# A factorization network for 2048 rows: layer 0's last tile halved and stacked, tile kinds and side work at other steps

## The chip, the cores and the metric

One core of a Trainium2 chip. The time is the device time of one execution in microseconds; the number compared is the median over several executions. Engines: TensorE (PE; PEld are its weight loads), VectorE (DVE), ScalarE (ACT), GpSimd (POOL), and SyncE (SP), which here only issues DMAs.

## The reference, cut to what matters

39 embedding tables are looked up for 2048 batch rows, 16 numbers each. Three layers (L0 to L2) then multiply every field of x0 with every field of xk and contract the pairs with a weight matrix; an MLP ends it.

```python
e = stack([tbl_f[ids[:, f]] for f in range(39)], axis=1)        # 2048 x 39 x 16
x0 = xk = e
for idx, (W, b) in enumerate([(w0, b0), (w1, b1), (w2, b2)]):   # W: 39 x fk x 128
    z = relu(einsum('bhd,bkd,hks->bsd', x0, xk, W) + b[None, :, None])
    if idx != 2:
        xk = z[:, :64, :]; direct.append(z[:, 64:, :])
    else:
        direct.append(z)
h = concatenate([sum(concatenate(direct, axis=1), axis=-1), dense_ctx], axis=1)
h = relu(h @ W_top1 + b_top1); h = relu(h @ W_top2 + b_top2); y = h @ W_top3
```

## The kernel before

**Turns and tiles.** A turn works on 128 batch rows and 8 of the 16 channels, so on 1024 columns; there are 32 turns (CHUNKS), two to a group of 128 rows. A tile is a block of up to 128 pair products (partitions) by 1024 columns; TensorE contracts it with a 128 x 128 block of weights into PSUM, in two halves of 512 columns. A turn has 47 steps, one tile each: steps 0 to 19 (PAIRED) are layer 1, steps 20 to 26 (SQUARED) are layer 0 of the turn that follows, steps 27 to 46 (LAST) are layer 2. All engines walk through the same list of steps (`turns`, L195), each emitting what it has to do at each step; the semaphores alone decide when it happens.

**Kinds.** The string PLAN (L58) gives each tile a letter. F: the fp32 product goes to TensorE as it is (L1014). V, D and P tiles are split: ScalarE rounds the product into `high` (L801), the rest `low = product - high` is subtracted by VectorE (V, D; L869) or by POOL (P; L638), and TensorE does three contractions, low weights by high, high weights by high (`contract`, L1014) and, LATE = 2 steps later, high weights by low (`contract_low`, L1049). The product of a D tile is made in PSUM, in the bank of the other accumulator; that of V and P tiles in SBUF. A V tile of 64 rows is stacked: its high part stands in partitions 0 to 63 and its low part in 64 to 127 of one buffer, its weights are there twice, and two contractions do for three, both two steps late (L1046, L1049). Before the change the stacked tiles are 19 and 46.

**Products (VectorE).** In layers 1 and 2 a product is a spread tile of x0 (SBUF) by the maps of the layer before (PSUM); two neighbours are made in one instruction where the plan allows (`pairs`; L914), else one (L918). Layer 0 is symmetric, so only shifts are needed: row s + 3 i of tile 20 + u is field i - s by field i + 3 u (L899), 117 rows a tile. Its 20 shifts fill 7 tiles, the last with two shifts. `prod` has 8 buffers and `high` has 4, so a product waits for TensorE's work on the tile 8 before.

**Side work at fixed steps.** The relus (`take`): layer 0 at RELU0_AT = 29, layer 1 at 21, each in three parts (L741 to L743), layer 2 at 3 (L725). The pair 27/28 needs relu 1, tile 0 of the next turn needs relu 0. The channel sums of `direct` (L925, L929, L936), three steps each: layers 0 and 1 from SUM01_AT = 27, layer 2 from SUM2_AT = 14. The low part of a V tile is emitted SUB = 3 steps after its product, that of a D tile SUB_D = 2. POOL also gathers table rows (L616), at steps that `gather_slots` spreads over those that are not P. In even turns TensorE transposes gathered rows at step 13 (L1056).

**Loads (SP).** `load_spread` (L540) fills the spread tiles in layer 2's steps; `load_first` at step 46 fills x_thrice (L530) and the first four `shifted` buffers (L518); tiles 24 to 26 of layer 0 are loaded into freed buffers (L518; L522 for the last one, two loads of 39 rows). In the start-up `load_thrice0` and `load_shifted0` do this in parts, as blocks of rows are written to DRAM.

Of the kernel before, what the change touches and what calls it, by code (L numbers as in the profile page):

```python
# [29 lines left out]
MAPS = 128  # L30
# [9 lines left out]
N0 = -(-SHIFTS // PER0)  # L40
N1 = -(-FIELDS // 2)
TILES = N1 + N0 + N1
TRIPLE = FIELDS * PER0
PERIODS = 2
# [13 lines left out]
PLAN = "FVFPPPFPFFDPFDVFFPFV" "FFFFFFF" "FPFFFVPFDPVFDPPDFPFV"  # L58
# [32 lines left out]
def shifts_of(u):  # L91

    return min(PER0, SHIFTS - PER0 * u)
# [115 lines left out]
def build(nc, a, out):  # L209
# [10 lines left out]
    with ctx:  # L220
# [27 lines left out]
        with nc.sbuf_tensor("shifted_r", [TRIPLE, RING0, COLS], f32r) as shifted_r, \  # L248
                nc.sbuf_tensor("x_thrice_r", [TRIPLE, COLS], f32r) as x_thrice_r:
            pass  # L250
        shifted = sb("shifted", [TRIPLE, RING0, COLS])
        x_thrice = sb("x_thrice", [TRIPLE, COLS])
# [33 lines left out]
        s_thrice = sem("s_thrice")  # L286
        s_shifted = [sem(f"s_shifted{u}") for u in range(N0)]
# [108 lines left out]
        w0_other = prod[0:TRIPLE, 4, 0:N0 * MAPS].rearrange("p (t s) -> p t s", s=MAPS)  # L396
# [85 lines left out]
        def _(sp):  # L482
# [5 lines left out]
            sp.dma_start(w_plain[0:TRIPLE, plan_f - PLAIN0:plan_f, :], a["w0_ab"][:, 0:PLAIN0, :]).then_inc(s_w0, 16)  # L488
            sp.dma_start(w0_other, a["w0_ba"]).then_inc(s_w0, 16)
            if PARTED0:  # L490
                sp.dma_start(parts_in[0:TRIPLE, plan_r - PARTED0:plan_r, :], a["w0_ab"][:, PLAIN0:N0, :]).then_inc(s_w0, 16)
# [23 lines left out]

            def load_shifted(n, u):
                if shifts_of(u) == PER0:
                    sp.dma_start(shifted[:, u % RING0, :], period(n, PER0 * u, FIELDS).unsqueeze(1).to_broadcast(  # L518
                        [FIELDS, PER0, COLS])).then_inc(s_shifted[u], 16)
                    return  # L520
                for s in range(shifts_of(u)):
                    sp.dma_start(shifted[s:TRIPLE - PER0 + s + 1:PER0, u % RING0, :], period(n, PER0 * u, FIELDS)  # L522
                                 ).then_inc(s_shifted[u], 16)
# [19 lines left out]
            for q in range(TURNED):  # L543
                sp.wait_ge(s_first_w[q], 16 * PERIODS)
                if q < FIRST_PARTS:
                    for piece in EARLY_PIECES[q]:
                        load_spread(Turn(None, 0), piece)
                else:
                    load_thrice0(sp, q - FIRST_PARTS)
                    for u in () if q == TURNED - 1 else range(RING0):  # L550
                        load_shifted0(sp, u, q - FIRST_PARTS)

# [133 lines left out]
        def _(act):  # L686
# [21 lines left out]
            if PARTED0:  # L708
                act.wait_ge(s_prep, 1)
                nc.scalar.activation(w_high[0:TRIPLE, parts12:plan_r, :], parts_in[0:TRIPLE, parts12:plan_r, :], ACT.Copy  # L710
                                     ).then_inc(s_cast, 1)
# [132 lines left out]
        def _(dve):  # L844
            nc.vector.memset(sums[:, :, :, :], 0.0)

            dve.wait_ge(s_first_g[-1], 16 * len(BLOCKS[-1]))
            dve.wait_ge(s_w0, 16 * (3 if PARTED0 else 2))
            squares = w_plain[0:TRIPLE, plan_f - PLAIN0:plan_f, :]
            done = nc.vector.tensor_tensor(squares, squares, w0_other[:, 0:PLAIN0, :], ALU.add)  # L850
            parts12 = plan_r - PARTED0
            if PARTED0:
                squares = parts_in[0:TRIPLE, parts12:plan_r, :]
                done = nc.vector.tensor_tensor(squares, squares, w0_other[:, PLAIN0:N0, :], ALU.add)
# [4 lines left out]
            if PARTED0:  # L859
                dve.wait_ge(s_cast, 2)  # L860
                nc.vector.tensor_tensor(w_low[0:TRIPLE, parts12:plan_r, :], parts_in[0:TRIPLE, parts12:plan_r, :],
                                        w_high[0:TRIPLE, parts12:plan_r, :], ALU.subtract).then_inc(s_prep, 1)
# [8 lines left out]
            def product(turn, j):  # L871
# [19 lines left out]
                if j in SQUARED:  # L891
                    u, nxt = j - N1, turn.shift(1)
                    if u == 0 and turn.fixed and turn.number() == -1:
                        dve.wait_ge(s_prep, 3 if PARTED0 else 2)
                    if u == 0:
                        dve.wait_ge(s_thrice, nxt.count(16 * PER0, 16 * PER0 + EXTRA_THRICE))
                    loads = 1 if shifts_of(u) == PER0 else shifts_of(u)
# [97 lines left out]
        def _(pe):  # L995
# [38 lines left out]

            def contract_low(turn, j):
# [42 lines left out]
            def emit(turn, j):  # L1078
# [75 lines left out]
def laid_out(given):  # L1154
# [11 lines left out]
    ab, ba = np.zeros((TRIPLE, N0, MAPS), np.float32), np.zeros((TRIPLE, N0, MAPS), np.float32)  # L1166
    for n, j in enumerate(SQUARED_ORDER):
        u, i = j - N1, np.arange(FIELDS)
        for s in range(shifts_of(u)):
            f, g = (i - s) % FIELDS, (i + PER0 * u) % FIELDS  # L1170
            ab[s::PER0, n] = w0[f, g]
            if (u, s) != (0, 0):
                ba[s::PER0, n] = w0[g, f]
# [28 lines left out]
```

## Time and profile before

| | us |
|---|---|
| median of 3 runs (lowest, highest) | 2503.74 (2494.42, 2505.49) |
| profiled execution, its own time | 2490.02 |
| its span | 2488.2 |
| TensorE busy | 2399.6 |
| VectorE busy | 2240.9 |
| POOL busy | 1679.1 |
| ScalarE busy | 1058.4 |
| mean granted TensorE clock | 0.996 of full |

The span runs from the first to the last instruction of one execution. Busy time is the union of an engine's instructions. In a timeline a row is a run of equal instructions: start, length, engine, line, what is written and read, how many, and in brackets the idle time ahead with what ended it. Ends of matmuls are modelled, so costs on TensorE are better read from one start to another.

### The profile page before, as it was taken

The page shows a single profiled execution, that of the slowest core. Times are in us where ns is not written, and L with a number is a line of the kernel's source. Part 1 is how long each engine was busy: PE and PEld are TensorE (multiplying, and loading weights), DVE is VectorE, ACT ScalarE, POOL GpSimd, SP SyncE. Part 2 cuts the span into 40 slices and gives each one's busy share as a digit, 9 for nine tenths or more (in the row PEclk, how much of TensorE's full clock was granted, in tenths as well). Part 3 has the DMA queues.
Part 4 walks back from the last instruction along what each step waited for, and adds up shares of the span by engine and source line. Part 5 has one row for each costly group of instructions (what it writes and reads, how often), then busy time and mean ns, then how long its engine had stood idle before and what let it go on. Part 6 is the DMA issues. An engine that isn't in the chain of part 4 may idle for free. (4 is left out here: it accounts for less than half of the span.)

```text
span 2488.2 us, 29429 instructions
## 1 busy us (share of the span) xinstructions
PE 2399.6 (96%) x7702; PEld 1442.7 (58%) x7702; DVE 2240.9 (90%) x1657; ACT 1058.4 (43%) x1053; POOL 1679.1 (67%) x1059
## 2 busy tenths in 40 slices
PE   0899999999999999999999999999999999999989
PEld 0465555665565666556556655656665555665556
DVE  0799998999999999999999999999999998999993
ACT  0244443444444444444444444443444443444445
POOL 7877766767677676777767677776768767544340
PEclk9999999999999999999999999999999999999999
DMA  6888787998778789888779887888988777888730
GB/s 162 203 197 196 193 191 183 208 215 191 190 199 191 196 212 213 189 190 199 191 196 216 207 190 187 201 192 197 215 210 188 192 197 173 210 205 195 182 79 11
DMA packets 172546, 469.79 MB, mean 189 GB/s; under 512 B 28987, under 2 KB 63163, under 8 KB 172245
## 3 DMA queue, kind: packets, MB, share of 16 engines
q1 hardware_dynamic: 148869, 461.35, 76.7%
q0 software_dynamic: 19968, 5.15, 2.2%
q10 hardware_dynamic: 3680, 2.95, 0.5%
q8 instruction: 13, 0.21, 0.0%
q14 instruction: 16, 0.12, 0.0%
HBM read 457.02 MB, written 12.33 MB: 189 GB/s over the span
## 5 line engine op out<-in xcount | busy, mean ns | idle before, releaser
L638 POOL TENSOR_TENSOR low<-prod,high 128x1024 fp32r<-128x1024 f32 x384 | 945.9, 2473 | 553.7 <-ACT high L801 551.2
L914 DVE TENSOR_TENSOR prod<-spread,maps 128x2048 f32<-128x2048 f32 x448 | 1016.7, 2281 | 72.8 <-ACT direct L743 20.9
L801 ACT ACTIVATE high<-prod 128x1024 fp32r<-128x1024 f32 (+1 forms) x576 | 596.2, 1056 | 715.9 <-DVE prod L914 458.4
L616 POOL DMA_INDIRECT landed<-in_tbl,rows_id x585 | 620.6, 1061 | 165.6 <-issue 148.6
L1014 PE MATMUL zacc_a<-prod,w_plain 128*128 128x512 f32 (+1 forms) x1536 | 709.1, 596 | 17.0 <-DVE prod L899 11.1
L1014 PE MATMUL zacc_b<-prod,w_plain 128*128 128x512 f32 (+1 forms) x1536 | 706.2, 594 | 5.9 <-DVE prod L914 5.9
L1014 PEld LDWEIGHTS zacc_a<-prod,w_plain 128*128 128x128 f32 (+1 forms) x1536 | 291.9, 190 | 288.9 <-issue 259.9
L1014 PEld LDWEIGHTS zacc_b<-prod,w_plain 128*128 128x128 f32 (+1 forms) x1536 | 291.2, 190 | 275.0 <-issue 246.8
L899 DVE TENSOR_TENSOR prod<-shifted,x_thrice 117x1024 f32<-117x1024 f32 x224 | 266.7, 1230 | 66.8 <-DMA shifted<-x_periods 53.7
L1049 PE MATMUL zacc_b<-low,w_high 128*128 128x512 f32 x672 | 281.2, 499 | 6.2 <-POOL low L638 6.2
L1049 PE MATMUL zacc_a<-low,w_high 128*128 128x512 f32 x672 | 280.7, 498 | 0.7 <-DVE low L869 0.5
L918 DVE TENSOR_TENSOR prod<-spread,maps 128x1024 f32<-128x1024 f32 (+1 forms) x224 | 265.4, 1208 | 0.0
L1014 PE MATMUL zacc_b<-high,w_low 128*128 128x512 f32 x672 | 237.6, 434 | 1.8 <-ACT high L801 1.7
L1014 PE MATMUL zacc_a<-high,w_low 128*128 128x512 f32 x672 | 238.3, 436 | 0.1
L1014 PE MATMUL zacc_a<-high,w_high 128*128 128x512 f32 x672 | 211.3, 395 | 0.0
L1014 PE MATMUL zacc_b<-high,w_high 128*128 128x512 f32 x672 | 211.3, 395 | 0.0
L1049 PEld LDWEIGHTS zacc_b<-low,w_high 128*128 128x128 f32 x672 | 127.1, 190 | 105.9 <-issue 83.7
L1049 PEld LDWEIGHTS zacc_a<-low,w_high 128*128 128x128 f32 x672 | 126.8, 189 | 100.4 <-issue 77.5
L869 DVE TENSOR_TENSOR low<-prod,high 128x1024 fp32r<-128x1024 f32 x128 | 165.0, 1289 | 0.0
L1014 PEld LDWEIGHTS zacc_b<-high,w_low 128*128 128x128 f32 x672 | 126.3, 189 | 59.2 <-issue 31.0
L1014 PEld LDWEIGHTS zacc_a<-high,w_low 128*128 128x128 f32 x672 | 125.7, 189 | 53.9 <-issue 30.7
L1014 PEld LDWEIGHTS zacc_a<-high,w_high 128*128 128x128 f32 x672 | 126.5, 188 | 29.9
(103 smaller groups left out, 1618.9 us busy)
## 6 DMA issues: line engine op xcount, KB each, us to landing
spread<-x_periods SPq DMA_DIRECT2D x608, 512.0 KB, 16.5
shifted<-x_periods SPq DMA_DIRECT2D x188, 468.0 KB
x_thrice<-x_periods SPq DMA_DIRECT2D x93, 156.0 KB
shifted<-x_periods SPq DMA_DIRECT2D x64, 156.0 KB
landed<-in_tbl,rows_id POOLq DMA_INDIRECT x585, 4.6
spread<-x_periods SPq DMA_DIRECT2D x32, 256.0 KB, 20.7
x_periods<-x SPq DMA_DIRECT2D x30, 256.0 KB, 2.2
spread<-features SPq DMA_DIRECT2D x4, 512.0 KB, 4.6
```

The lines of the kernel that those rows point to most:

```text
L616: nc.gpsimd.indirect_dma_start(out=landed[:, f, :], out_offset=None, in_=tables[f], in_offset=bass.IndirectOffsetOnAxis(ap=rows[:, f:f + 1 ...
L638: nc.gpsimd.tensor_tensor(low[0:rows, at_, :], prod[0:rows, at_, :], high[0:rows, slot(j, SPLIT, NH), :], ALU.subtract).then_inc(s_lowp, 1)
L801: nc.scalar.activation(high[0:rows, h, :], made(turn, j)[0:rows, :], ACT.Copy).then_inc(s_round, 1)
L869: nc.vector.tensor_tensor(to, whole, top, ALU.subtract).then_inc(s_lowv, 1)
L899: nc.vector.tensor_tensor(to, shifted[0:rows, u % RING0, :], x_thrice[0:rows, :], ALU.mult).then_inc(s_square, 1)
L914: nc.vector.tensor_tensor(prod[:, at_:at_ + 2, :], spread[:, t:t + 2, :], maps[:, :].unsqueeze(1).to_broadcast([128, 2, COLS]), ALU.mult). ...
L918: nc.vector.tensor_tensor(to, spread[0:rows, t, :], maps[0:rows, :], ALU.mult).then_inc(s_prod, 1)
L1014: return nc.tensor.matmul(z[:, hf * BANK:(hf + 1) * BANK], w, x[:, hf * BANK:(hf + 1) * BANK], start=start, stop=stop)
L1049: done = nc.tensor.matmul(z[:, cols], w_high[0:rows, r, :], x[:, cols], start=False, stop=last)
```

## The change

Layer 0's seven tiles become six full ones and a half one. The 11 partitions that were free in each of tiles 20 to 23 (SPARE) take 44 of the 78 pairs of the last two shifts (SPARE_SHIFTS); the 34 others fit into 40 rows of tile 26, which now has 64 rows, kind V, and so is stacked. Its second operand is a buffer of its own, x_last, of which partitions 32 to 63 are zeroed once at the start (s_zero). Each turn loads 11 more rows into x_thrice and into four shifted buffers, and for tile 26 four loads of 20 rows instead of two of 39. A step at which TensorE issues nothing (`silent`: step 26) has its count added by the step before.

The plan and the places:

```diff
-PLAN = "FVFPPPFPFFDPFDVFFPFV" "FFFFFFF" "FPFFFVPFDPVFDPPDFPFV"
+PLAN = "FPFVPFFPDFPPDPVDFVFV" "FFFFFFV" "FFFVFFPFFPDFPDFPDPFV"
-RELU0_AT, RELU1_AT, RELU2_AT = N1 + N0 - 1 + 3, N1 - 1 + 2, 3
-SUB, SUB_D = 3, 2
+RELU0_AT, RELU1_AT, RELU2_AT = N1 + N0 - 1 + 4, N1 - 1 + 1, 5
+SUB, SUB_D = 2, 2
-SUM01_AT, SUM2_AT = 27, 14
+SUM01_AT, SUM2_AT = 28, 21
```

The half tile:

```diff
+SPARE = ROWS - TRIPLE
+SPARE_SHIFTS = (19, 18, 20, 21)
+LAST_RUN, LAST_GAPS = 10, ((19, 11, 20), (18, 11, 21))
...
     if j in SQUARED:
-        return TRIPLE
+        return HALF if j == SQUARED[-1] else ROWS if j - N1 < len(SPARE_SHIFTS) else TRIPLE
...
+def loads_of(u):
+    return 4 if u == N0 - 1 else 2 if u < len(SPARE_SHIFTS) else 1
...
+        x_last = sb("x_last", [HALF, COLS])
...
+            if part == 0:
+                engine.dma_start(x_thrice[TRIPLE:ROWS, :], chunk0(0, SPARE)).then_inc(s_thrice, 16)
...
+            if part == 1:
+                engine.dma_start(shifted[TRIPLE:ROWS, u, :], chunk0(SPARE_SHIFTS[u], SPARE)).then_inc(s_shifted[u], 16)
...
+            def load_last(n, to, second):
+                for i, (shift, first, gap) in enumerate(LAST_GAPS):
+                    rows = period(n, first + (shift if second else 0), 2 * gap).rearrange("(b t) c -> t b c", b=2)
+                    sp.dma_start(to[2 * LAST_RUN * i:2 * LAST_RUN * (i + 1), :], rows[0:LAST_RUN, :, :]
+                                 ).then_inc(s_shifted[N0 - 1], 16)
...
+                if u < len(SPARE_SHIFTS):
+                    sp.dma_start(shifted[TRIPLE:ROWS, u % RING0, :], period(n, SPARE_SHIFTS[u], SPARE)
                                  ).then_inc(s_shifted[u], 16)
...
+                sp.dma_start(x_thrice[TRIPLE:ROWS, :], period(n, 0, SPARE)).then_inc(s_thrice, 16)
                 for u in range(RING0):
                     load_shifted(n, u)
+                load_last(n, x_last, False)
...
+            nc.vector.memset(x_last[HALF // 2:HALF, :], 0.0).then_inc(s_zero, 1)
...
-                    nc.vector.tensor_tensor(to, shifted[0:rows, u % RING0, :], x_thrice[0:rows, :],
+                    nc.vector.tensor_tensor(to, shifted[0:rows, u % RING0, :], (x_last if u == N0 - 1 else x_thrice)[0:rows, :],
                                             ALU.mult).then_inc(s_square, 1)
...
+            def silent(j):
+                return j < TILES and stacked(j) and PLAN[j - LATE] not in SPLIT
...
-                    done.then_inc(s_mm, 1)
+                    if not silent(j):
+                        done.then_inc(s_mm, 2 if silent(j + 1) else 1)
```

The weights of layer 0 get 128 instead of 117 rows, with those of the moved pairs in their new rows and zeros where a row of tile 26 repeats a pair.

## Rows read from the trace of the kernel before

**Rows 1.** The page's head and its part 1: busy time, share, instructions.
```profile
span 2488.2 us, 29429 instructions
PE 2399.6 (96%) x7702; PEld 1442.7 (58%) x7702; DVE 2240.9 (90%) x1657; ACT 1058.4 (43%) x1053; POOL 1679.1 (67%) x1059
```

**Rows 2.** Waits of TensorE and VectorE: us in total, times, longest.
```profile
PE zacc_b L1049 <- POOL low L638: 6.2, 2, 3.8
DVE prod L899 <- DMA shifted<-x_periods: 53.7, 41, 3.2
```

**Rows 3.** Timeline of ScalarE, relu of layer 2 in three turns in a row.
```profile
609.26 1.11 ACT L725 ACTIVATE direct<-zacc_a,bias 128x1024 f32<-128x1024 f32 x1 [1.36 <-PE zacc_a L1049]
681.69 1.11 ACT L725 ACTIVATE direct<-zacc_b,bias 128x1024 f32<-128x1024 f32 x1 [1.43 <-PE zacc_b L1049]
754.68 1.11 ACT L725 ACTIVATE direct<-zacc_a,bias 128x1024 f32<-128x1024 f32 x1 [1.37 <-PE zacc_a L1049]
```

**Rows 4.** Timeline of TensorE in the turn from 1145.
```profile
1149.48 8.75 PE L1014 MATMUL zacc_b<-prod,w_plain 117*128 117x512 f32 x20
1158.07 1.88 PE L1014 MATMUL zacc_a<-prod,w_plain 128*128 128x512 f32 x4
...
1176.27 0.62 PE L1014 MATMUL zacc_a<-high,w_low 128*128 128x512 f32 x2
...
1181.38 1.88 PE L1014 MATMUL zacc_a<-prod,w_plain 128*128 128x512 f32 x4
```

**Rows 5.** Timeline of VectorE in the same turn, from tile 27 to tile 27.
```profile
1153.08 2.29 DVE L914 TENSOR_TENSOR prod<-spread,maps 128x2048 f32<-128x2048 f32 x1
...
1158.54 0.79 DVE L936 TENSOR_TENSOR sums<-direct 128x128 f32<-128x128 f32 x1
...
1172.03 2.29 DVE L914 TENSOR_TENSOR prod<-spread,maps 128x2048 f32<-128x2048 f32 x1 [0.38 <-PE zacc_a L1049]
...
1183.82 4.49 DVE L914 TENSOR_TENSOR prod<-spread,maps 128x2048 f32<-128x2048 f32 x2 [0.39 <-issue]
...
1203.87 2.29 DVE L914 TENSOR_TENSOR prod<-spread,maps 128x2048 f32<-128x2048 f32 x1 [0.60 <-PE zacc_b L1049]
...
1213.94 3.53 DVE L899 TENSOR_TENSOR prod<-shifted,x_thrice 117x1024 f32<-117x1024 f32 x3
...
1222.32 2.36 DVE L899 TENSOR_TENSOR prod<-shifted,x_thrice 117x1024 f32<-117x1024 f32 x2 [1.21 <-DMA shifted<-x_periods]
1225.44 2.29 DVE L914 TENSOR_TENSOR prod<-spread,maps 128x2048 f32<-128x2048 f32 x1 [0.76 <-PE zacc_a L1014]
```

**Rows 6.** Lines L869, L936 (durations ns min/median/max) and a group of L801 (mean ns).
```profile
L869 DVE TENSOR_TENSOR low<-prod,high x128: 1209/1217/3404, 91.8 to 2416.2; 128x1024 fp32r<-128x1024 f32 x128
L869 DVE TENSOR_TENSOR low<-zacc_b,high x80: 1209/1217/1222, 102.6 to 2351.0; 128x1024 fp32r<-128x1024 f32 x80
...
L869 DVE TENSOR_TENSOR high<-prod,high x64: 1208/1219/1256, 119.0 to 2427.1; 64x1024 fp32r<-64x1024 f32 x64
...
L936 DVE TENSOR_TENSOR sums<-direct x64: 281/322/2036, 132.9 to 2432.3; 128x128 f32<-128x128 f32 x64
...
L801 ACT ACTIVATE high<-prod 64x1024 fp32r<-64x1024 f32 x64 | 67.9, 1061 | 158.2 <-DVE prod L918 120.6 <-POOL low L638 37.6
```

**Rows 7.** Windows of layers 2, 1, 0: us, busy of PE, PEld, DVE, ACT, POOL; clock, DMA.
```profile
1158.07:1187.14 29.07, 29.07 (x100) 18.47 (x98) 28.26 (x21) 15.34 (x15) 23.15 (x16) 1.00 1.04 221
1187.14:1217.45 30.31, 30.31 (x101) 18.85 (x100) 29.62 (x22) 11.74 (x12) 23.76 (x15) 1.00 0.80 206
1217.45:1230.41 12.96, 12.96 (x34) 6.07 (x33) 10.89 (x10) 4.32 (x4) 6.90 (x8) 1.00 0.41 116
```

**Rows 8.** Timeline of ScalarE, the last part of relu 1.
```profile
1224.20 1.11 ACT L743 ACTIVATE direct<-zacc_b,bias 64x1024 f32<-64x1024 f32 x1
```

**Rows 9.** Timeline of SP's queue in the start-up.
```profile
55.46 2.83 SPq L472 DMA_DIRECT2D shifted<-x_periods  x4
59.43 3.39 SPq L466 DMA_DIRECT2D x_thrice<-x_periods  x5
```

More of the change, by code:

```diff
@@ L40 @@
 N0 = -(-SHIFTS // PER0)
+assert SHIFTS == PER0 * (N0 - 1) + 2
 N1 = -(-FIELDS // 2)
@@ L85, in rows_of, with last_pairs @@
     if j in SQUARED:
-        return TRIPLE
+        return HALF if j == SQUARED[-1] else ROWS if j - N1 < len(SPARE_SHIFTS) else TRIPLE
     t = j if j in PAIRED else j - N1 - N0
     return HALF * min(2, FIELDS - 2 * t)
-def shifts_of(u):
-    return min(PER0, SHIFTS - PER0 * u)
+def loads_of(u):
+    return 4 if u == N0 - 1 else 2 if u < len(SPARE_SHIFTS) else 1
+def last_pairs():
+    taken = {min((r, (r + e) % FIELDS), ((r + e) % FIELDS, r)) for r in range(SPARE) for e in SPARE_SHIFTS}
+    for n, (shift, first, gap) in enumerate(LAST_GAPS):
+        for t in range(LAST_RUN):
+            for b in range(2):
+                f = first + gap * b + t
+                g = (f + shift) % FIELDS
+                once = f < FIELDS and min((f, g), (g, f)) not in taken
+                yield 2 * LAST_RUN * n + 2 * t + b, f % FIELDS, g, once
 def stacked(j):
@@ L247, in build @@
         x = sb("x", [128, TURNED, ROWS])
-        with nc.sbuf_tensor("shifted_r", [TRIPLE, RING0, COLS], f32r) as shifted_r, \
-                nc.sbuf_tensor("x_thrice_r", [TRIPLE, COLS], f32r) as x_thrice_r:
-            pass
-        shifted = sb("shifted", [TRIPLE, RING0, COLS])
-        x_thrice = sb("x_thrice", [TRIPLE, COLS])
+        with nc.sbuf_tensor("shifted_r", [ROWS, RING0, COLS], f32r) as shifted_r, \
+                nc.sbuf_tensor("x_thrice_r", [ROWS, COLS], f32r) as x_thrice_r:
+            pass
+        shifted = sb("shifted", [ROWS, RING0, COLS])
+        x_thrice = sb("x_thrice", [ROWS, COLS])
+        x_last = sb("x_last", [HALF, COLS])
         direct01 = sb("direct01", [128, COLS])
@@ L514, in period @@
                 return flat[first:first + rows, n.odd * COLS:(n.odd + 1) * COLS]
+            def load_last(n, to, second):
[3 more added lines that the diff above has]
+                                 ).then_inc(s_shifted[N0 - 1], 16)
             def load_shifted(n, u):
-                if shifts_of(u) == PER0:
-                    sp.dma_start(shifted[:, u % RING0, :], period(n, PER0 * u, FIELDS).unsqueeze(1).to_broadcast(
-                        [FIELDS, PER0, COLS])).then_inc(s_shifted[u], 16)
+                if u == N0 - 1:
+                    load_last(n, shifted[:, u % RING0, :], True)
                     return
-                for s in range(shifts_of(u)):
-                    sp.dma_start(shifted[s:TRIPLE - PER0 + s + 1:PER0, u % RING0, :], period(n, PER0 * u, FIELDS)
+                sp.dma_start(shifted[0:TRIPLE, u % RING0, :], period(n, PER0 * u, FIELDS).unsqueeze(1).to_broadcast(
+                    [FIELDS, PER0, COLS])).then_inc(s_shifted[u], 16)
+                if u < len(SPARE_SHIFTS):
+                    sp.dma_start(shifted[TRIPLE:ROWS, u % RING0, :], period(n, SPARE_SHIFTS[u], SPARE)
                                  ).then_inc(s_shifted[u], 16)
@@ L551, in _ @@
                         load_shifted0(sp, u, q - FIRST_PARTS)
+            sp.wait_ge(s_zero, 1)
+            load_last(Turn(None, 0), x_last, False)
             def load_context():
@@ L852, in _ @@
             if PARTED0:
-                squares = parts_in[0:TRIPLE, parts12:plan_r, :]
+                squares = parts_in[:, parts12:plan_r, :]
                 done = nc.vector.tensor_tensor(squares, squares, w0_other[:, PLAIN0:N0, :], ALU.add)
@@ L1164, in tile @@
         return np.concatenate([rows, rows]) if stacked(j) else rows
-    ab, ba = np.zeros((TRIPLE, N0, MAPS), np.float32), np.zeros((TRIPLE, N0, MAPS), np.float32)
+    ab, ba = np.zeros((ROWS, N0, MAPS), np.float32), np.zeros((ROWS, N0, MAPS), np.float32)
     for n, j in enumerate(SQUARED_ORDER):
         u, i = j - N1, np.arange(FIELDS)
-        for s in range(shifts_of(u)):
+        if u == N0 - 1:
+            for row, f, g, once in last_pairs():
+                if once:
+                    ab[row::HALF, n], ba[row::HALF, n] = w0[f, g], w0[g, f]
+            continue
+        for s in range(PER0):
             f, g = (i - s) % FIELDS, (i + PER0 * u) % FIELDS
-            ab[s::PER0, n] = w0[f, g]
+            ab[s:TRIPLE:PER0, n] = w0[f, g]
             if (u, s) != (0, 0):
-                ba[s::PER0, n] = w0[g, f]
+                ba[s:TRIPLE:PER0, n] = w0[g, f]
+        if u < len(SPARE_SHIFTS):
+            f = np.arange(SPARE)
+            g = (f + SPARE_SHIFTS[u]) % FIELDS
+            ab[TRIPLE:, n], ba[TRIPLE:, n] = w0[f, g], w0[g, f]
     given["w0_ab"], given["w0_ba"] = ab, ba
```

20 lines of the change are left out of this document (11 added, 9 removed).

## The prediction

> **What bounds the kernel now.** I read the page's busy shares first: TensorE 96%, VectorE 90% [rows 1], then the waits of TensorE: beside those of the start-up and the last turn only single waits on POOL's low parts remain, the longest 3.8 us [rows 2]. So the steady part is a full TensorE stream. The starts of layer 2's relu give its beat: 72.43 and 72.99 us for two turns in a row [rows 3]; even turns carry the extra transposes of the gathered rows, worth 0.56 us. What a tile costs is read from starts, as matmul durations overlap. Five plain F tiles take 1158.07 - 1149.48 = 8.59 us, 1.718 each. Between 1176.27 and 1181.38 lie eleven pairs of rounded matmuls (one pair covers both column halves): 0.4645 each [rows 4]. A split tile is three pairs, 1.394; a stacked one two, 0.929. A turn has 24 F, 21 split and 2 stacked tiles: 41.2 + 29.3 + 1.9 = 72.4, the beat. VectorE is close behind. From the doubled product that opens layer 2 (1153.08) to the next one (1225.44) it has idles of 0.38, 0.39, 0.60, 1.21 and 0.76, in all 3.34 of 72.36 us [rows 5]: 69.0 us of work.
>
> **The change, part by part.**
>
> (a) *Tile 26.* Layer 0's last tile goes from F (1.718) to stacked (0.929): -0.789 us of TensorE a turn. Fewer rows alone would bring nothing: at 1.718 for the F tiles of 128 rows too, layer 2 comes to 8 x 1.718 + 11 x 1.394 = 29.08, as measured [rows 7]. The kind does it. The first layer 0 lies in the start-up, 31 are in the steady stream: -24.5 us, as long as TensorE stays fed.
>
> (b) *Kinds of the other 40 tiles.* F stays 17, split 21, stacked 2, so no TensorE time, but two F leave layer 1 and two enter layer 2. P falls from 12 to 11, D rises from 5 to 6.
>
> (c) *VectorE.* It gains tile 26's subtraction (1.219 in its stacked form) and that of the D (1.217, from PSUM) [rows 6]: +2.44 a turn. Doubled products stay 14 (8 and 6 become 7 and 7), 0. The channel sum's third step took 0.79 [rows 5] against a median of 0.32 [rows 6]. I lay the rest on POOL, which subtracts tile 28 just then; layer 2's first P is tile 33 now: 0 to -0.47, taken as -0.4. Sum: 69.0 + 2.0 = 71.1 against a TensorE beat of 71.6 and 72.2. The margin falls from 3.3 us a turn to some 0.8. This is where the change can fail, so I go through the stages.
>
> Layer 2: TensorE 29.07 [rows 7] + 2 x (1.718 - 1.394) + 0.93 (tile 26's matmuls fall at step 28) = 30.65. VectorE 1183.82 - 1153.08 less 0.38 and 0.39 = 29.97, five subtractions before and after, -0.4: 29.6. VectorE gains 1.1. Layer 1: TensorE 30.31 - 0.65 = 29.66 (30.22 in even turns). VectorE 1213.94 - 1183.82 - 0.60 = 29.52, + 2.44 for two more subtractions (seven for five), -1.2 as the layer 2 sum leaves for layer 0: 30.8. It loses 1.1 or 0.5. Layer 0: TensorE 12.96 - 1.72 = 11.24. VectorE 1225.44 - 1213.94 - 1.21 - 0.76 = 9.53, + 1.2 for the sum = 10.7. It gains 0.5.
>
> The idle of 1.21 is a wait for a shifted load [rows 5]. The three sum steps and the small last load stand just there, so I let the wait go; what is late next is relu 1. Its last part ends at 1225.31, 7.86 us after TensorE entered layer 0 at 1217.45; only then can the pair 27/28 be multiplied, 2.2 us more, 10.1 in all [rows 5, 8]. TensorE asked for tile 27 at 12.96 [rows 7]; now it asks at 11.24. The lead there falls from 2.8 to 1.1 us, still positive. RELU1_AT moves past steps in which ScalarE has nothing, 0.
>
> (d) *ScalarE.* One more rounding a turn, 1.06 us [rows 6] on an engine 43% busy [rows 1], 0: relu 1 is through before tile 26's product. Relu 0 now waits for step 28 (3.44 + 0.93 = 4.4 us into layer 2), takes three parts of 1.11 [rows 8], ends at 7.8 and holds the rounding of tile 33, which TensorE wants at 10.9: covered by 2 us. Relu 2 (1.11 [rows 3]) moves two steps later and has tile 8's PSUM product behind it. TensorE gives it its sums at 1.72 + 2 x 0.93 = 3.6 us into layer 1, so it is done by 5 to 7. VectorE, 1.1 ahead at the entry, reaches tile 8 after three doubled products and two subtractions, at 3 x 2.2 + 2 x 1.2 - 1.1 = 7.9. So 0, and if this cover is gone, 1 us a turn.
>
> (e) *POOL.* One subtraction less, and at most two P tiles in a row (10, 11) where there were three (3, 4, 5): 0.
>
> (f) *SP and the DMAs.* Each turn: five loads of 11 rows and four of 20 rows instead of two of 39, some 0.23 MB more. The queue is busy 0.80 of layer 1's stretch [rows 7], mostly ahead of the first square: 0. In the start-up four more issues stand ahead of the last x_thrice part: SP ended the four before at 58.29 and issued the next at 59.43 [rows 9]; 4 x 0.71 more end at 61.1, +1.7. Then tile 26's product passes through rounding, subtraction and matmuls, 1.06 + 1.22 + 0.93 = 3.2, where the F form took 1.7 or more: 0 to +1.6, and 0.3 taken, since TensorE has six other tiles to work off. Together +2.0 (bounds 0 to 4).
>
> (g) *SUB from 3 to 2.* The low part of a V is made one product earlier; the rounding needs 1.06 and a doubled product, 2.28, lies between in most places. 0, at worst 0.1 a turn. SUM01_AT moves with relu 0: 0.
>
> (h) *Stalls that come with the thin margin.* The trace before shows none. Below: 0. Above: the 1.2 us DMA wait in every turn. I take 0.15 a turn, near the low end, since all three stage entries keep a positive lead: 31 x 0.15 = +4.6.
>
> **Sum:** -24.5 + 2.0 + 4.6 = -17.9. The profiled execution took 2490.0 us, its span of 2488.2 [rows 1] and 1.8 around it: 2472. The median of the runs shown lies 13.7 above it, which the trace cannot explain, so I carry it: 2503.7 - 17.9 = 2486.
>
> **Rivals.**
>
> *A, the whole gain:* no stalls, start-up +1. -24.5 + 1 gives 2480, and beside a run like the lowest shown (2494) 2471. For it: the ledger closes with 0.8 us to spare. Against: that spare is thinner than the jitter of the DMA wait (1.21 here, 53.7 over 41 waits [rows 2]).
>
> *B, VectorE becomes the bound (within 0.5%):* if the shifted wait stays, VectorE needs 71.1 + 1.2 + 0.4 (the idle at tile 0) = 72.7, the beat of before. Nothing is gained but the start-up's 2 lost: 2506, or with half the turns hit 2494. Against: the sum steps now fill the place of the wait.
>
> *C, slower:* the place is the entry of layer 2, tile 27. If the last load and relu 1 both come late there, TensorE waits in each turn by what VectorE passes the old beat. A beat of 73.2 instead of 72.7 costs 31 x 0.5 = +15.5, with the start-up's 2 it gives 2521. It decides from 1.6 us of new VectorE waits a turn. For it: squares, stacked subtractions and sums read two SBUF tensors, and such a subtraction took up to 3.40 us, while those with one operand in PSUM never passed 1.22 [rows 6]; a block by POOL costs up to 2.2 us, and one in every turn would be enough. Against: a POOL subtraction lies beside few of the new places, and there is one less.
> The Trainium skill (SBUF — State Buffer, "Who interferes with whom") says a DVE instruction with two SBUF inputs contends with a GpSimd instruction that reads SBUF, and whoever issues first blocks the other for its whole instruction. The trace agrees by these maxima. By that rule the stacked subtraction and the layer 2 sum, now among squares, are exposed to POOL's SBUF reads and the PSUM one is not; it is case C if they meet each turn.
>
> *D, the change does not do what it says:* if tile 26 were not stacked, its matmuls would remain four F ones and the time near 2504. The code gives it 64 rows and kind V, so this has no chance of note.
>
> **Numbers.** A measurement of this kernel tells about 0.5%, 12.5 us, from no change. My forecast, in which TensorE stays the bound with few stalls: 0.42, own range 2476 to 2494. A: 0.20. B: 0.24. C: 0.14. The forecast stays below 2491 in most of its range. Faster: 0.36 + 0.19 + 0.03 = 0.58; same: 0.06 + 0.01 + 0.19 + 0.03 = 0.29; slower: 0.02 + 0.11 = 0.13. The range runs from 2465 (A beside a low run) to 2512, which leaves out most of C.
>
> **What would show it.** Right: two turns' beats of 71.6 and 72.2; VectorE busy 93% or more; the shifted wait gone from most turns; six F tiles of layer 0 in 10.3 us, then layer 2 at once; relu 0 starting some 4.5 us into layer 2. Wrong: waits of TensorE on VectorE's products at tile 27 or 0 in every turn; the shifted wait still above 1 us; relu 2 or relu 0 followed by waiting roundings; VectorE subtractions of 2 us and more at tile 26, or a start-up longer by over 4 us.

## The result and the profile after

The changed kernel takes 2619.86 us (median of 4 runs, 2617.43 to 2622.15) against 2503.7 for the kernel before in the same comparison: a ratio of 1.0467, 95% interval [1.0446, 1.0489]. It is slower by 4.7%. The forecast was 2486 in a range of 2465 to 2512, with 0.13 for slower: sign and range are both wrong, and no rival named what happened.

The head of the page of the changed kernel, its part 1, and one of its rows of DMA queues (packets, MB, share):

```profile
span 2615.6 us, 30319 instructions
PE 2418.2 (92%) x7700; PEld 1456.0 (56%) x7700; DVE 2288.4 (87%) x1724; ACT 1101.0 (42%) x1086; POOL 1584.9 (61%) x1027
...
q14 instruction: 80, 0.66, 0.1%
```

VectorE works 47.5 us more than in [rows 1] (2288.4 for 2240.9), 1.5 a turn where 2.0 was priced, and its busy share falls all the same: both VectorE and TensorE now idle. The queue q14 carried 16 packets and 0.12 MB before. The waits (us in total, times, longest) say where the time is:

```profile
DVE prod L950 <- issue: 91.5, 30, 6.8
...
DVE low L905 <- issue: 70.6, 13, 5.6
PE zacc_a L1050 <- ACT high L836: 69.3, 13, 5.6
PE zacc_a L1050 <- DVE prod L950: 33.6, 22, 10.5
DVE prod L935 <- DMA shifted<-x_periods: 16.6, 22, 2.0
```

The wait for shifted loads of [rows 2] did shrink, 53.7 to 16.6. In its place stand two idles of over 5 us that wait for nothing that the profile shows ("issue"), 13 times each: 13 of the 30 ahead of L950, and all 13 ahead of L905. The timeline of VectorE where they fall:

```profile
855.84 1.22 DVE L905 TENSOR_TENSOR high<-prod,high 64x1024 fp32r<-64x1024 f32 x1
857.20 2.29 DVE L950 TENSOR_TENSOR prod<-spread,maps 128x2048 f32<-128x2048 f32 x1
866.29 2.29 DVE L950 TENSOR_TENSOR prod<-spread,maps 128x2048 f32<-128x2048 f32 x1 [6.80 <-issue]
874.03 1.23 DVE L905 TENSOR_TENSOR low<-prod,high 128x1024 fp32r<-128x1024 f32 x1 [5.45 <-issue]
```

The pair comes back every two turns, 13 times (401.50, 556.00, 710.45, 866.29 and so on to 2267.79), never in between. The first of each takes 5.86 to 6.80 us, the second 5.29 to 5.59; all 26 together are 153.9 us. Two turns are one pass of the hardware loop, which starts three steps into layer 1 and is run 14 times, so that it has 13 back edges; a turn is otherwise the same code. So the idles hang on the loop's back edge (the branch from its end to its start), not on the data. Layer 2's relu gives the beat:

```profile
1102.63 1.11 ACT L760 ACTIVATE direct<-zacc_a,bias 128x1024 f32<-128x1024 f32 x1
1180.90 1.10 ACT L760 ACTIVATE direct<-zacc_b,bias 128x1024 f32<-128x1024 f32 x1
1258.39 1.10 ACT L760 ACTIVATE direct<-zacc_a,bias 128x1024 f32<-128x1024 f32 x1
```

78.27 and 77.49 us, where [rows 3] had 72.43 and 72.99. TensorE, which waits 5.62 us behind 864.3, then has a granted clock of 0.50 (1.2 GHz) from 870 to 875 and 1.00 (2.4 GHz) again from 876 on; over the whole run it is 0.977 for 0.996.

What differs at the back edge is the length of the code. Counted in the built program, VectorE's loop body has 274 instructions after the change and 255 before. Only four of the 19 more compute (the two new subtractions of each turn); 13 are register arithmetic, by which a looped kernel works out the values that its waits compare with. The other engines' bodies changed too (SP 157 to 182, ScalarE 220 to 228, TensorE 516 to 520, POOL 97 to 93) and show no such idle once a pass. ScalarE has 13 "issue" idles ahead of a relu (L776; 88.3 us in all, the longest 9.5), but not once a pass, and the fast run with 6 memsets below has 18 of them.

**Theory T, code loading.** VectorE's instructions would come in blocks of 256, of which two are held. The back edge would find the first block gone when the body touches three; it would stall there, and again where the next block begins. The second idle falls four or five instructions behind the loop's first one, so that one stands near place 252 of its block: 252 + 274 = 526, three blocks. Before, ten fewer instructions stand ahead of the loop, so it starts near 242: 242 + 255 = 497, two. The Trainium skill (Runtime: NRT & Kernel Launch, "Instruction fetch mechanics") states such blocks, two of them held, and a stall at a taken branch to a target outside; of crossing a boundary it says that the cost is "mostly hidden". The trace agrees with the first. It does not agree with the second where the crossing comes four or five instructions behind the branch, 5.45 us; the crossing in the middle of the body, by the same count, shows no such idle.
**Rival W.** The idles are waits whose record the trace lacks: the later relu places, the new loads, or the thin margin of the prediction's case C.

### The profile page after: what moved, and what is told of

It reads as the page before. It is cut to its first block and busy times, and to the rows that moved or that the text cites. A ratio compares the mean times of both kernels' runs of the same rounds, so it can differ in the third digit from the quotient of the medians.

```text
span 2615.6 us, 30319 instructions
## 1 busy us (share of the span) xinstructions
PE 2418.2 (92%) x7700; PEld 1456.0 (56%) x7700; DVE 2288.4 (87%) x1724; ACT 1101.0 (42%) x1086; POOL 1584.9 (61%) x1027
## 5 line engine op out<-in xcount | busy, mean ns | idle before, releaser
L673 POOL TENSOR_TENSOR low<-prod,high 128x1024 fp32r<-128x1024 f32 x352 | 842.0, 2397 | 748.0 <-ACT high L836 744.9
L950 DVE TENSOR_TENSOR prod<-spread,maps 128x2048 f32<-128x2048 f32 x448 | 1019.4, 2279 | 107.4 <-issue 91.5
L836 ACT ACTIVATE high<-prod 128x1024 fp32r<-128x1024 f32 (+1 forms) x576 | 607.1, 1059 | 1074.6 <-DVE prod L950 662.8
L651 POOL DMA_INDIRECT landed<-in_tbl,rows_id x585 | 678.3, 1159 | 175.4 <-issue 164.2
L1050 PE MATMUL zacc_b<-prod,w_plain 128*128 128x512 f32 (+1 forms) x1472 | 675.1, 593 | 7.0 <-DVE prod L950 6.9
L1050 PEld LDWEIGHTS zacc_b<-prod,w_plain 128*128 128x128 f32 (+1 forms) x1472 | 278.5, 189 | 268.3 <-issue 240.6
L1089 PE MATMUL zacc_a<-low,w_high 128*128 128x512 f32 x672 | 271.5, 489 | 4.6 <-DVE low L905 4.6
L1089 PE MATMUL zacc_b<-low,w_high 128*128 128x512 f32 x672 | 271.4, 488 | 4.3 <-POOL low L673 4.3
L935 DVE TENSOR_TENSOR prod<-shifted,x_thrice 128x1024 f32<-128x1024 f32 (+1 forms) x192 | 230.6, 1215 | 39.0 <-issue 19.7
L1050 PE MATMUL zacc_b<-high,w_low 128*128 128x512 f32 x672 | 230.4, 424 | 0.0
L954 DVE TENSOR_TENSOR prod<-spread,maps 128x1024 f32<-128x1024 f32 (+1 forms) x192 | 229.4, 1208 | 0.0
L905 DVE TENSOR_TENSOR low<-prod,high 128x1024 fp32r<-128x1024 f32 x128 | 157.8, 1233 | 70.6 <-issue 70.6
```

The source lines that it names most:

```text
L651: nc.gpsimd.indirect_dma_start(out=landed[:, f, :], out_offset=None, in_=tables[f], in_offset=bass.IndirectOffsetOnAxis(ap=rows[:, f:f + 1 ...
L673: nc.gpsimd.tensor_tensor(low[0:rows, at_, :], prod[0:rows, at_, :], high[0:rows, slot(j, SPLIT, NH), :], ALU.subtract).then_inc(s_lowp, 1)
L836: nc.scalar.activation(high[0:rows, h, :], made(turn, j)[0:rows, :], ACT.Copy).then_inc(s_round, 1)
L905: nc.vector.tensor_tensor(to, whole, top, ALU.subtract).then_inc(s_lowv, 1)
L935: nc.vector.tensor_tensor(to, shifted[0:rows, u % RING0, :], (x_last if u == N0 - 1 else x_thrice)[0:rows, :], ALU.mult).then_inc(s_square, 1)
L950: nc.vector.tensor_tensor(prod[:, at_:at_ + 2, :], spread[:, t:t + 2, :], maps[:, :].unsqueeze(1).to_broadcast([128, 2, COLS]), ALU.mult). ...
```

## The experiments

The kernel before took 2487.6 us beside the first four runs, 2507.9 beside the next four and 2505.1 beside the last four; these are different chips, so kernels are compared by their ratios to it.

**Code loading, from both kernels.** One-element memsets ahead of the loop on VectorE move the loop's place and do nothing else (they fall into VectorE's wait for the gathered rows, which lasts until 55 us):

```diff
+            for n in range(12):
+                nc.vector.memset(filler[0:1, n:n + 1], 0.0)
```

> The changed kernel with 12 one-element memsets more at the start of VectorE's program, where it waits for gathered rows until 55 us anyway; nothing else differs. Theory T (code loading): VectorE's loop body has grown from 255 to 274 instructions and now starts just ahead of a border between two blocks of code, so that each pass of the loop (two turns) must load code twice; the trace of the changed kernel shows both places in every pass, a 6.5 us and a 5.4 us idle put down to issue, and 0.66 MB on the instruction queue instead of 0.12. Twelve instructions more ahead of the loop move its start behind the border: both idles vanish, the instruction queue goes back to about 0.12 MB, and of 13 x 11.7 = 152 us nearly all comes back: 2465 to 2490. Rival W (the thin margin: VectorE's new work and waits make TensorE wait): the time stays at 2616 to 2622, or grows by the 0.8 us of the memsets.

Measured: 2458.16 us, ratio 0.9888 [0.9872, 0.9905]. The changed kernel, with 12 useless instructions added, is 29.4 us faster than before, and 7 below the range that T gave. Its page and its VectorE waits:

```profile
span 2454.6 us, 30331 instructions
PE 2366.9 (96%) x7700; PEld 1442.4 (59%) x7700; DVE 2286.4 (93%) x1736; ACT 1100.1 (45%) x1086; POOL 1575.4 (64%) x1027
...
q14 instruction: 15, 0.12, 0.0%
```

```profile
DVE prod L938 <- DMA shifted<-x_periods: 25.8, 29, 3.8
...
DVE prod L953 <- issue: 9.0, 17, 1.7
```

The work is the same (2286.4 for 2288.4 us), the idles are gone.

The same from the other side: ten one-element memsets in each turn of the kernel before (275 instructions in the body), once with 10 and once with 30 ahead of the loop.

```diff
+                if not turn.fixed and j in range(0, 20, 2):
+                    nc.vector.memset(filler[0:1, 40 + j + turn.odd:41 + j + turn.odd], 0.0)
```

> The kernel before with 20 one-element memsets in VectorE's loop body (10 a turn, 275 instructions in all) and 10 ahead of the loop, so that the loop starts at the place where that of the changed kernel starts. No plan, load or place is changed. T: the same two idles of some 6 us in each of 13 passes, less the 3.3 us a turn by which VectorE was ahead: 2590 to 2640. W: VectorE had 3.3 us a turn to spare and gets 10 x 0.07 = 0.7 us more: 2490 to 2510, as before.

> As the run before it, with 30 instead of 10 memsets ahead of the loop: body and work in the loop are the same to the instruction, the loop only starts 20 instructions later. T: the border is passed, no idles on issue, 2490 to 2510. W and every theory by the amount of work: the same time as the run before it, within 2 us.

Measured: with 10 ahead 2649.86 us, ratio 1.0656 [1.0638, 1.0673]; with 30 ahead 2490.51, ratio 1.0008 [0.9998, 1.0018]. The same instructions cost 159 us more in one place than in the other, where they cost 3, in a kernel that has none of the change's tiles, loads or places. The first lies 10 above T's range of 2590 to 2640. The page and a wait of the slow one:

```profile
q14 instruction: 80, 0.66, 0.1%
...
DVE filler L955 <- issue: 69.7, 13, 5.5
```

W has fallen: waits that hang on the work, the loads or the margin would not go with the place of the code.

**The border.** The changed kernel with 3 and with 6 memsets ahead.

> The changed kernel with 3 one-element memsets ahead on VectorE; the loop, 274 VectorE instructions long, then starts some 255 instructions into a block of 256 by the place of the second stall (estimate; without the memsets some 252). Code loading by blocks of 256: the body still touches three blocks, so the time stays near the changed kernel's, 2600 to 2625 us, with some 80 packets on the instruction queue of VectorE. Rival, any shift by a few instructions helps (a matter of timing, not of a border): 2455 to 2500 us. The start-up: if the 10 us later first square of the changed kernel comes back with it, it belongs to the kernel; if it starts at 66 to 67 us, it was that execution's own and the time is some 10 us lower.

> The same with 6 memsets ahead; the loop then starts behind the border (2 or so into the next block) and ends 276 into it, two blocks. Code loading by blocks of 256: 2455 to 2462 us as with 12 memsets, some 16 packets on the instruction queue. Rival, that the border is elsewhere or that there is none: near 2615 us, or something between.

Measured: 3 ahead, 2677.08 us, ratio 1.0673 [1.0655, 1.0691]; 6 ahead, 2469.43, ratio 0.9841 [0.9825, 0.9858]. Three instructions decide 208 us, between the places that the position of the second idle gave. The run with 6 lies above its 2455 to 2462, on a chip where the kernel before is 20 us slower. The run with 3 misses in size: by the changed kernel's ratio 2625 was to come on this chip, and it is 52 more. With 3, both idles fall together, as the loop's first instruction is then the last or so of its block, and the one that is left takes 13.78 to 14.58 us, where the two took 11.8 in the mean; that gives 31 of the 52, and the rest was not traced. The timelines of VectorE and of TensorE:

```profile
893.85 2.29 DVE L953 TENSOR_TENSOR prod<-spread,maps 128x2048 f32<-128x2048 f32 x1 [13.96 <-issue]
```

```profile
897.44 1.22 PE L1053 MATMUL zacc_a<-high,w_low 128*128 128x512 f32 x2 [13.00 <-ACT high L837]
898.46 1.05 PE L1053 MATMUL zacc_a<-high,w_high 128*128 128x512 f32 x2
899.31 3.62 PE L1053 MATMUL zacc_a<-prod,w_plain 128*128 128x512 f32 x4
...
903.45 1.88 PE L1053 MATMUL zacc_a<-prod,w_plain 128*128 128x512 f32 x4
```

The windows around it (us, busy of PE, PEld, DVE, ACT, POOL; granted clock, DMA share, GB/s):

```profile
882.00:897.00 15.00, 2.43 (x9) 1.32 (x7) 3.15 (x2) 0.67 (x1) 0.00 (x0) 0.75 1.00 217
897.00:900.00 3.00, 2.56 (x5) 1.82 (x6) 3.00 (x3) 1.75 (x3) 2.39 (x1) 0.50 0.82 281
900.00:903.00 3.00, 3.00 (x5) 1.29 (x4) 3.00 (x3) 1.73 (x3) 2.23 (x1) 0.50 0.85 273
903.00:906.00 3.00, 3.00 (x10) 1.76 (x10) 2.08 (x3) 1.80 (x2) 2.01 (x2) 0.95 0.63 204
```

After 13.00 us of idleness, within which the granted clock has fallen (0.75 in the mean from 882 to 897), TensorE runs at 0.50, 1.2 GHz, and four plain matmuls take 3.62 us for 1.88. The DMA engines are fully busy (1.00) while VectorE waits for its code; that the two code blocks queue behind that traffic would explain 5 to 7 us for each, but no run varied the traffic, so it stays open.

What these runs show is that the place of the code alone decides, that the border lies within three instructions, and that the idles come with more packets on the instruction queue. All places here fit theory T's blocks of 256 with two held; the size itself is taken from the page of the Trainium skill cited there (Runtime: NRT & Kernel Launch, "Instruction fetch mechanics"), as no run measures it alone. No run has a body short enough for two blocks that starts just ahead of the border, so it is not shown that the length of 274 is needed beside the place.

**The start-up.** In the changed kernel's trace the first square starts at 75.69 us, before at 65.83. I tried whether the new 11-row loads do it, by moving the shifted ones to ScalarE's queue:

```diff
-            if part == 1:
+            if part == 2:
                 engine.dma_start(shifted[TRIPLE:ROWS, u, :], ...
```

> The padded changed kernel (12 memsets) with the four 11-row loads into the shifted buffers of the start-up given to ScalarE's queue, behind the last part, instead of SP's queue ahead of the last x_thrice part. In the changed kernel that part was issued at 69.9 us instead of 59.4, and the first square started at 75.7 instead of 65.8. If the interleaved small loads hold SP's queue: the first square is back near 66 to 68 us and the time 6 to 10 us below the padded kernel. If it is the whole amount of data that is late: no more than 2 us.

Measured: 2457.26 us, ratio 0.988 [0.9863, 0.9896], no different from 2458.16. A miss: there was nothing to gain, as the first square of the padded kernel already starts at 66.91 on this chip, and with the loads moved at 65.70. The kernel before with fillers has it at 66.44 and 65.48 there, so the change's own share is 0.5 to 1.4 us. What makes the start late elsewhere stays open. It is not the chip alone. With the same loads the first square starts at 72.77 to 77.30 in the four traces of the next chip, and at 69.00, 72.37, 76.23 and 76.94 in the four of the last. SP's queue took 2.01 us for three x_thrice issues in all four traces of the first chip, but on each of the others both 2.01 and 4.7 to 6.0 (5.32 in the changed kernel's trace).

**What the change is worth, with the code in place.** From here all kernels have 12 memsets ahead and two-block bodies (15 packets on q14 in each). First tile 26 back to F:

```diff
-"FFFFFFV"
+"FFFFFFF"
```

> The changed kernel with 12 memsets ahead, but tile 26 of kind F again (four plain matmul passes, no rounding, no low part); everything else as changed. Body of 268 VectorE instructions, two blocks. Step (a): each turn's TensorE time grows by 0.79 us, beats of 72.4 and 73.0, 24.5 us more than with the half tile, a ratio of 0.994 to 1.000 to the kernel before. Rival, the new places alone carry the gain: ratio below 0.990. Rival, the kind brings more than its matmuls: above 1.003.

Measured: 2501.48 us, ratio 0.9988 [0.9979, 0.9998]. Without the half tile the new places bring 0.1%. Its beats are 72.73 and 73.45, 73.09 in the mean. The changed kernel with 12 ahead (the run with 6 has the same) comes to 72.0 in the mean of all turns, and its undisturbed pairs are 72.24 and 71.53, 71.9 in the mean:

```profile
1107.52 1.10 ACT L761 ACTIVATE direct<-zacc_b,bias 128x1024 f32<-128x1024 f32 x1
1179.76 1.10 ACT L761 ACTIVATE direct<-zacc_a,bias 128x1024 f32<-128x1024 f32 x1
1251.29 1.10 ACT L761 ACTIVATE direct<-zacc_b,bias 128x1024 f32<-128x1024 f32 x1
```

That is 1.2 us a turn where 0.79 was priced; the rest is this comparison's own, as its tile 26 is an F tile of 64 rows. The five F tiles that end layer 0 take 8.87 us in it (1231.79 to 1240.66), where [rows 4] has 8.59. Read at three moments, the timeline of TensorE there:

```profile
1238.23 1.22 PE L1053 MATMUL zacc_a<-prod,w_plain 117*128 117x512 f32 x2
1238.75 1.98 PE L1053 MATMUL zacc_a<-prod,w_plain 64*128 64x512 f32 x4
1240.66 1.12 PE L1053 MATMUL zacc_b<-prod,w_plain 128*128 128x512 f32 x2
```

The last matmul of 117 rows takes 0.52 us from its start to the next instead of 0.43, the first of 64 rows 0.53, the two after it 0.43; the same comes once more on the way back to 128 rows. So it is not the 64 rows that are dear, but each change of the number of rows to or from 64, two matmuls by some 0.1 us each. That is 0.39 us a turn, in all 32 turns of this trace, and 1.2 - 0.39 leaves 0.8.

Next the half tile alone: kinds of layers 1 and 2, low parts, relus 1 and 2 and the layer 2 sum as before; then the same with the sum at step 21.

```diff
-PLAN = "FPFVPFFPDFPPDPVDFVFV" "FFFFFFV" "FFFVFFPFFPDFPDFPDPFV"
+PLAN = "FVFPPPFPFFDPFDVFFPFV" "FFFFFFV" "FPFFFVPFDPVFDPPDFPFV"
-RELU0_AT, RELU1_AT, RELU2_AT = N1 + N0 - 1 + 4, N1 - 1 + 1, 5
-SUB, SUB_D = 2, 2
-SUM01_AT, SUM2_AT = 28, 21
+RELU0_AT, RELU1_AT, RELU2_AT = N1 + N0 - 1 + 4, N1 - 1 + 2, 3
+SUB, SUB_D = 3, 2
+SUM01_AT, SUM2_AT = 28, 14
```

> The half tile alone: tile 26 stacked, all other kinds and the places of low parts, relu 1, relu 2 and the layer 2 sum as in the kernel before (relu 0 one step later, as tile 26's matmuls need it, and the other sum with it), with 12 memsets ahead. Body of 260 VectorE instructions, two blocks. Term (a) alone: 2487.6 - 24.5 = 2463, 2460 to 2472 with the shifted wait. If the new places of the change carry a good part of its gain: 2470 to 2490. If they carry none: within 3 us of 2458.

> The run with the half tile alone (1.0133), with the layer 2 sum at step 21. If the sum's place is what the half tile needs, the shifted wait shrinks to 20 us in all and the beats go to 71.6 to 72.3: ratio 0.984 to 0.990. If the kinds of layers 1 and 2 are needed as well, because stacked subtractions stay long beside POOL (1470 ns against 1221): beats of 72.6 to 73.2, ratio 0.995 to 1.008.

Measured: 2542.79 us, ratio 1.0133 [1.0116, 1.015], and 2540.27, ratio 1.0146 [1.0125, 1.0166]. Both expectations are missed, on the high side; the second named the stacked subtractions that stay long beside POOL, which they do (1467 ns), but beats of 72.6 to 73.2, where most are 73.2 to 74.2. The half tile in the old places makes the kernel slower than before, and moving the sum alone does not mend it. In both, TensorE waits for a stacked subtraction once a turn, in the mean 1.15 us. TensorE's waits with the sum at 21 (us in total, times, longest):

```profile
PE zacc_b L1089 <- DVE high L908: 20.1, 17, 1.8
PE zacc_a L1089 <- DVE high L908: 16.8, 15, 1.7
```

With the changed kernel's places and 12 memsets ahead these two waits come to 2.5 us in all. The tile is 26: with SUB = 3 its subtraction is emitted behind the product of step 29, and TensorE wants it at step 28 (LATE = 2). It meets POOL there besides: at 1265.57 it starts behind the pair 29/30 and takes 2.59 us, and TensorE waits 1.69.

Then the changed kernel with one place of before at a time: the layer 2 sum at step 14, and low parts of kind V three tiles behind (SUB = 3).

> The changed kernel with 12 memsets ahead and the layer 2 sum back at step 14. Step (c) of the prediction: the wait for a shifted load comes back, about 1.2 us in many turns, and VectorE's margin of 0.8 us a turn goes, so TensorE waits in part of the turns: 2462 to 2475 us. Rival, VectorE has enough slack at the entry of layer 2 in any case: within 3 us of 2458. With it slower than 2490 the margin would be of a size that the ledger does not have.

> The changed kernel with 12 memsets ahead and the low parts of kind V three tiles behind, as before, instead of two. Step (g) gave this 0 to 0.1 us a turn: ratio within 0.002 of the padded changed kernel's 0.984 to 0.989, beats of 71.5 to 72.2. Rival, the distance decides which VectorE instruction meets POOL's: subtractions of 1.3 us mean and more, or the sum's second step near 1.0 us as in the run with the sum at 14; beats of 73 and more, ratio above 1.0.

Measured: sum at 14, 2534.34 us, ratio 1.0109 [1.0092, 1.0126]; SUB = 3, 2532.74, ratio 1.0114 [1.0097, 1.0131]. Each costs 2.3 to 2.8% and turns gain into loss; most beats are 73.4 to 74.8 and 73.7 to 73.9. The first is far above its range, beyond even the 2490 at which its text says that the margin must be of another size; in the second the rival holds. The groups by form (busy, mean ns | idle before) show one VectorE operation stretched in each. The sum's second step with the sum at 14, then in the run with 6 ahead:

```profile
L968 DVE TENSOR_TENSOR direct<-direct 128x256 f32<-128x256 f32 x64 | 64.5, 1008 | 0.0
```

```profile
L968 DVE TENSOR_TENSOR direct<-direct 128x256 f32<-128x256 f32 x64 | 26.8, 419 | 0.1
```

The subtractions with SUB = 3, then with 6 ahead:

```profile
L908 DVE TENSOR_TENSOR low<-prod,high 128x1024 fp32r<-128x1024 f32 x128 | 203.9, 1593 | 0.0
```

```profile
L908 DVE TENSOR_TENSOR low<-prod,high 128x1024 fp32r<-128x1024 f32 x128 | 157.8, 1233 | 0.0
```

And in the half tile with the sum at 21, squares and stacked subtractions (1214 and 1221 ns with 6 ahead):

```profile
L938 DVE TENSOR_TENSOR prod<-shifted,x_thrice 128x1024 f32<-128x1024 f32 x128 | 186.0, 1473 | 19.4 <-DMA x_thrice<-x_periods 18.4 <-DMA shifted<-x_periods 1.0
...
L908 DVE TENSOR_TENSOR high<-prod,high 64x1024 fp32r<-64x1024 f32 x96 | 140.8, 1467 | 4.2 <-ACT high L837 1.2
```

The timelines of POOL and of VectorE with SUB = 3 show how:

```profile
1220.81 2.40 POOL L674 TENSOR_TENSOR low<-prod,high 128x1024 fp32r<-128x1024 f32 x1 [2.81 <-ACT high L837]
```

```profile
1221.60 2.69 DVE L908 TENSOR_TENSOR low<-prod,high 128x1024 fp32r<-128x1024 f32 x1
```

POOL is through at 1223.21, and VectorE's instruction ends at 1224.29, 1.08 later: about its usual 1.22, so it got nearly nothing done beside POOL. With the sum at 14, POOL's subtraction of 1231.65 + 2.42 = 1234.07 stands beside a sum step of 1.92 us for 0.42 that starts at 1232.45. All of these read two tensors of SBUF. It is what the rule that case C quotes from the Trainium skill (SBUF — State Buffer, "Who interferes with whom") says, once in every turn. Counted over 200 to 2380 us: with the sum at 14, with SUB = 3 and in the last run below, 31, 31 and 30 two-tensor SBUF instructions of VectorE begin while over 0.3 us of a POOL subtraction is left, and every one takes over 0.15 us more than usual; with 6 ahead there is one. With the half tile alone and the sum at 21 it is 46 of 52. Of the 320 to 353 with an operand in PSUM that begin so in each run, none takes over 0.02 us more than usual.

With SUB = 3 the block is not all. It takes (203.9 - 157.8) / 32 = 1.4 us a turn of VectorE's time, but TensorE waits for something else more:

```profile
PE zacc_b L1089 <- DVE high L908: 15.0, 16, 3.5
PE zacc_a L1089 <- DVE high L908: 10.1, 19, 0.7
PE zacc_b L1092 <- DVE low L908: 3.9, 20, 0.7
```

The first two are stacked subtractions again, 35 waits, most of them for tile 46: in the turn shown its subtraction ends at 1217.17 and TensorE starts at 1217.22. The third holds the blocked ones. How the 1.9 us a turn splits between the block and low parts that come one product too late was not tested.

Last, a trial at more: tile 24 of kind P, to take 0.32 us more from TensorE with POOL's free time in layer 0.

```diff
-"FFFFFFV"
+"FFFFPFV"
```

> The changed kernel with 12 memsets ahead and tile 24, in layer 0, of kind P instead of F, rounded on ScalarE and subtracted on POOL, which has nothing in layer 0. TensorE 1.718 - 1.394 = 0.32 us less a turn, 10 us in all, if it is still the bound: beats of 71.2 and 71.8, ratio 0.980 to 0.985. Rival: VectorE, with 0.8 us to spare, now meets POOL's subtraction among the squares and becomes the bound: beats of 72.5 and more, squares above 1.3 us mean, ratio 0.990 to 1.010.

Measured: 2504.14 us, ratio 1.0002 [0.9992, 1.0011]. Ratio and beats (72.5 and 73.2) are the rival's, its mechanism only in part. The squares stay at 1213 ns; the stacked subtraction is caught, (1472 - 1221) x 96 / 32 = 0.75 us a turn:

```profile
L908 DVE TENSOR_TENSOR high<-prod,high 64x1024 fp32r<-64x1024 f32 x96 | 141.3, 1472 | 4.3 <-ACT high L837 1.4
```

But VectorE is not what TensorE waits for. It waits for ScalarE's rounding of tile 24, once in each of 31 turns:

```profile
PE zacc_b L1053 <- ACT high L837: 16.5, 16, 1.0
PE zacc_a L1053 <- ACT high L837: 15.4, 15, 1.0
```

That is 1.03 us a turn, three times what the tile was to save. In one turn the square is done at 1240.30, and ScalarE, busy with the three parts of relu 1 from 1239.57 on, rounds it from 1242.88. Neither the expectation nor its rival looked at what stands ahead of that rounding; whether the tile pays with relu 1 elsewhere was not tried.

So the best version found is the changed kernel with 6 or 12 instructions ahead of VectorE's loop, 1.1 to 1.6% below the kernel before.

## Why the prediction was wrong

**The step that failed is (c), VectorE's ledger.** It made a turn from the durations of the operations, "69.0 + 2.0 = 71.1", and took it that the engine is fed with instructions at no cost. The durations were right: with the memsets ahead VectorE is busy 93% and its turn fits into 71.9 us. But the kernel as changed needs 155.6 us for two turns in the mean, where the run with 12 ahead has 144.0: 11.6 us a pass, which is the two idles, 6.4 and 5.4 us in the mean, less a little that the margin took up. With 13 back edges that is 151 us, and the two ratios, 1.0467 and 0.984 to 0.989, lie 145 to 157 us apart. It is the whole miss: without it the forecast of 0.7% below the kernel before stands beside 1.1 to 1.6% measured. No rival named it, and no row of the kernel before shows such an idle. Neither the number of instructions in the loop body nor the place of the loop was looked at, although (b), (c) and (g) add subtractions to VectorE, and with them waits and their arithmetic.

(a) holds: 0.79 a turn was priced, and the undisturbed beats of the kernel before (72.43 and 72.99) and of the padded one (71.53 and 72.24) lie 0.82 apart; the two kinds of tile 26 give 0.8 as well, once the changes of row number are taken off. The forecast beats of 71.6 and 72.2 are met. "Fewer rows alone would bring nothing" was too kind: a 64-row F tile costs 0.39 more.

(c)'s smaller parts: VectorE's work grew by 1.5 us a turn, priced 2.0; the shifted wait goes from most turns (53.7 to 16.6 us), as said. The sum's move was priced as 1.2 us of wait alone; undone, it brings back both the wait (52.5 us in all) and a block by POOL, (64.5 - 26.8) / 32 = 1.2 us a turn, and the mean beat is 74.0, 2.0 more.

(g) was wrong by far: "at worst 0.1 a turn" for the low parts' distance, where SUB = 3 costs 1.9 a turn (mean beat 73.9). The term looked at whether the rounding is done in time. It looked neither at which POOL instruction the subtraction then meets nor at when TensorE wants a stacked tile's low part, two steps behind (LATE): the waits for stacked subtractions stand in all three runs with SUB = 3 (36.7, 36.9 and 25.1 us, against 2.5 in the padded kernel), at a VectorE that no longer runs ahead.

(b) and (e) at 0 fit the plan as it stands, which keeps VectorE's two-operand instructions off POOL's. The old kinds were only run together with SUB = 3 and the old relus (2.6 to 3.1% above the padded kernel), so what the kinds alone are worth is not shown.

(f): start-up +2.0 priced, 0.5 to 1.4 between traces of one chip, while the changed kernel's own trace starts 9.9 late for a reason that stays open. (h), 4.6 us of stalls: the padded kernel's mean beat of 72.0 lies 0.1 above its undisturbed pairs, 3 to 4 us in all; TensorE's waits for stacked subtractions are 2.5 of it.

Case C named the right weakness (1.6 us a turn of blocks and waits makes it slower): the run with the sum at 14 shows it, and the one with SUB = 3 shows it in part. It was not what made this kernel slow. Case A, the whole gain, is what the change gives when its code is in place: the forecast of 24.5 less the start-up against 29.4 on the first chip. Why it is 38 on another stays open.

## What to carry to other kernels

Count the instructions of each engine's loop body, waits and their register arithmetic included. By theory T, which fits every place tried here, a body of more than 256 instructions can touch three blocks, depending on where the loop starts, and then pays at each back edge. Idle instructions ahead of the loop settle it, 6 or 12 here; 3 made it worse. Its sign is an "issue" idle of several us, once in each pass, with more packets on the engine's instruction queue; an "issue" idle without these two is something else.

On a kernel whose VectorE is nearly full, place instructions with two SBUF operands against POOL's by the timeline: one meeting in every turn took 0.8 to 1.4 us of VectorE here, as much as the tile saved or more. And check for each rounded tile what stands ahead of its rounding and its subtraction on their engines at the step at which TensorE wants them: two of the losses above were such a wait.

## What the hardware showed that was not expected

- A back edge to a body of 274 instructions stalled VectorE twice, 5.9 to 6.8 and 5.3 to 5.6 us, or once for 13.8 to 14.6 us; with the loop three instructions further on there was no such stall. Each back edge brought five more packets on q14 (80 for 15, 13 back edges).
- After idles of 13.00 and of 5.62 us TensorE's granted clock was 0.50 for some 6 us.
- Matmuls of 64 rows took 0.43 us from start to start like those of 117 and 128, but each change to or from 64 rows cost two matmuls 0.1 us each, 0.39 us a turn.
- VectorE instructions with two SBUF operands that began beside a POOL subtraction were stretched in 92 cases of 92 in three runs (one of 1.22 us to 2.69, which ended 1.08 us after POOL's); those with an operand in PSUM in none of 320 to 353 a run.
- With the same start-up loads the first square started between 69.00 and 76.94 us in four traces of one chip.
